# Two cross-attention layers: the negation of the maxima, the image norms, the inverse norm and the mask moved between engines

## What is computed

```python
probs_t = softmax(einsum('bhsd,bhtd->bhst', q, k_t) * attn_scale)     # 371 text rows
attn_scores = einsum('bhsd,bhnd->bhsn', q, k_ip) * attn_scale         # 4 image rows
qsem = _l2norm(einsum('bhst,bte->bhse', probs_t, text_ehs))           # x / max(|x|, 1e-12)
ip_n = _l2norm(ip_ehs)
sem = einsum('bhse,bne->bhsn', qsem, ip_n)
probs_ip = softmax(attn_scores + 0.5 * sem) * spatial_mask[None, None, :, None]
ip_out = einsum('bhsn,bhnd->bhsd', probs_ip, v_ip)
out = (text_out + ip_out) @ W_out + b_out + residual
```

## Time and profile before

| what | value |
|---|---|
| median of 3 runs | 2812.94 us (2812.1 to 2813.39) |
| the profiled execution | 2810.17 us, of which the span from the first to the last instruction is 2808.4 us |
| PE (matmul) busy | 2666.7 us, 95% |
| DVE busy | 1709.4 us, 61% |
| ACT busy | 1253.6 us, 45% |
| POOL busy | 468.7 us, 17% |
| granted TensorE clock, mean | 0.988 |

### The profile page before, as it was taken

The page is one execution under the profiler, slowest core; times in us unless marked ns, Lnnn a source line. Parts: engine busy times, 40 slices in busy tenths (PEclk is TensorE's granted clock), DMA queues, the critical chain, the costliest instruction groups (busy, mean ns, idle before and its releaser), DMA issues.

```text
span 2808.4 us, 61414 instructions
## 1 busy us (share of the span) xinstructions
PE 2666.7 (95%) x25096; PEld 2083.7 (74%) x25096; DVE 1709.4 (61%) x3464; ACT 1253.6 (45%) x2265; POOL 468.7 (17%) x681
## 2 busy tenths in 40 slices
PE   6899999999999999999999999999999999999977
PEld 5677777777777777777777777777777777777755
DVE  3465666765666755666755666655666655667654
ACT  2344444444444444444444444444444444444443
POOL 1111121111121111121111111111111111111100
PEclk8999999999999999999999999999999999999988
DMA  7576546665546765546764556674557665567630
GB/s 196 97 85 87 83 80 83 90 85 84 84 78 84 93 85 81 82 76 90 88 90 79 83 77 86 83 98 76 82 80 88 84 91 80 83 83 85 85 35 7
DMA packets 450078, 236.31 MB, mean 84 GB/s; under 512 B 220459, under 2 KB 449787, under 8 KB 449788
## 3 DMA queue, kind: packets, MB, share of 16 engines
q1 hardware_dynamic: 433958, 209.34, 55.9%
q10 hardware_dynamic: 15840, 23.04, 2.7%
HBM read 166.38 MB, written 64.59 MB: 82 GB/s over the span
## 4 chain that ended last, share of the span: by engine, by line
PE 76%; DVE 13%; SPq 3%; ACT 3%; DMA 3%; issue 2%; POOL 0%; DVEq 0%; ACTq 0%; POOLq 0%
PE R L715 7%; PE ST L672 6%; PE R L569 5%; PE PN L689 5%; PE PN L745 5%; PE R L559 4%; PE R L616 4%; PE PN L732 4%; DVE m L899 4%; PE R L565 3%; PE R L718 3%; PE R L720 3%; PE R L629 3%; PE R L630 3%; PE R L766 2%
## 5 line engine op out<-in xcount | busy, mean ns | idle before, releaser
L1133 ACT ACTIVATE p<-ST 128x1344 f32<-128x1344 f32 x320 | 413.3, 1291 | 155.3 <-PE ST L675 149.5
L715 PE MATMUL R<-pr,Gh 128*128 128x448 f32 (+1 forms) x960 | 369.9, 385 | 28.4 <-DVE acc L801 28.4
L804 DVE SCALAR_TENSOR_TENSOR w<-p,pr 128x1344 f32<-128x1344 f32 x160 | 249.3, 1558 | 227.0 <-ACT pr L1148 227.0
L801 DVE TENSOR_TENSOR rem<-R,kst 128x375 f32<-128x375 f32 (+1 forms) x160 | 87.6, 547 | 485.2 <-ACT kst L1028 485.2
L801 DVE TENSOR_TENSOR w<-R,w 128x448 f32<-128x448 f32 (+1 forms) x480 | 290.7, 622 | 104.0 <-PE R L720 95.5
L629 PE MATMUL R<-wvh,ch 128*128 128x320 f32 (+3 forms) x896 | 302.8, 338 | 11.2 <-DVE cl L801 10.9
L630 PE MATMUL R<-wvh,cl 128*128 128x320 f32 (+3 forms) x896 | 279.6, 312 | 0.0
L672 PEld LDWEIGHTS ST<-Qs,Ks 100*128 100x128 bf16 (+1 forms) x3520 | 189.1, 98 | 88.0 <-issue 32.9
L1194 POOL TENSOR_TENSOR kst<-rem,kst 128x375 bf16<-128x375 f32 (+1 forms) x160 | 146.6, 916 | 618.7 <-ACT kst L1028 319.9
L672 PE MATMUL ST<-Qs,Ks 100*128 100x112 bf16 (+1 forms) x3520 | 228.7, 214 | 15.5 <-DMA Qs<-ms 6.8
L1148 ACT ACTIVATE pr<-ST 128x1344 fp32r<-128x1344 f32 x160 | 205.3, 1283 | 82.2 <-PE R L720 82.2
(11 more groups left out here) (178 smaller groups left out, 5761.7 us busy)
## 6 DMA issues: line engine op xcount, KB each, us to landing
Ks<-k_split SPq DMA_DIRECT2D x384, 140.6 KB, 6.4
k_split<-kst SPq DMA_DIRECT2D x128, 281.2 KB, 3.1
Ks<-k_split SPq DMA_DIRECT2D x384, 93.8 KB, 9.4
Qs<-q_split SPq DMA_DIRECT2D x384, 70.0 KB, 9.2
cT<-in_ctxT ACTq DMA_DIRECT2D x30, 750.0 KB, 4.7
q_split<-qst SPq DMA_DIRECT2D x128, 84.0 KB, 2.0
k_split<-kst SPq DMA_DIRECT2D x64, 140.6 KB, 2.9
xT<-in_xT SPq DMA_DIRECT2D x32, 192.0 KB, 3.2
```

The source lines that it names most:

```text
L715: e.matmul(r[0:nj, 0:QW], Gh[0:ROWS[u], q:q + nj], pr[0:ROWS[u], QW * u:QW * u + QW], start=u == 0, stop=False)
L801: return e.tensor_tensor(to, x, y, op)
L804: return e.scalar_tensor_tensor(out=to, in0=x, scalar=s, in1=y, op0=op0, op1=op1)
L1133: e.activation(p32[i][:].rearrange("p (u q) -> p u q", u=3), st, ACT.Exp).then_inc(p_whole, 1)
```

## The change

Four edits. (1) The stage's DVE instruction `m_neg` and the tile `mn` go; PE transposes `m0` or `m1` directly once the eighth reduction is done, and ACT's two copies scale by -1. (2) The inverse image norms are multiplied into the columns `g4` by POOL in stage `w4`, before ACT spreads them; DVE's multiplication L998 goes. (3) ACT's `Sqrt` and DVE's reciprocal L994 go; POOL raises `d2` to the power -0.5 in stage `ns_T`, and a constant factor moves into `ninv`. (4) Mask and inverse sum are applied in one `scalar_tensor_tensor`, and L1014 goes.

```diff
-                    w.wait_ge(m_neg, at("m_neg", b, l))
-                    e.transpose(R[slot["R", ("m_T", b, l)]][0:n, 0:S], mn[:, 0:n], ident[0:S, 0:S]).then_inc(m_T, 1)
+                    w.wait_ge(s_max_read, 8 * at("m_T", b, l))
+                    e.transpose(R[slot["R", ("m_T", b, l)]][0:n, 0:S], (m0, m1)[l][:], ident[0:S, 0:S]).then_inc(m_T, 1)
...
-                    e.tensor_scalar(nv, nv, 0.5, None, ALU.mult).then_inc(dve_step, own.one())
+                    e.tensor_scalar(nv, nv, 0.5 / math.sqrt(2.0), None, ALU.mult).then_inc(dve_step, own.one())
...
-                    if at("s_max", *key) > 8:
-                        w.wait_ge(m_neg, (at("s_max", *key) - 1) // 8)
+                    if h0 == 0 and ("m_T", (b - 1, l)) in o.nth:
+                        w.wait_ge(m_T, at("m_T", b - 1, l))
...
-                    e.tensor_scalar(mn[:, 0:n], m_[:], -1.0, None, ALU.mult).then_inc(m_neg, 1)
...
-                    w.wait_ge(d_root, b + 1)
-                    e.reciprocal(sm[0][:], d2[:]).then_inc(dve_step, own.one())
-                    w.wait_ge(dve_step, own.n)
-                    tt(f0[:], num[:], sm[0][:].unsqueeze(2).to_broadcast([S, H, NIP]), ALU.mult).then_inc(num_read, 1)
+                    w.wait_ge(d_inverse, b + 1)
+                    tt(f1[:], num[:], d2[:].unsqueeze(2).to_broadcast([S, H, NIP]), ALU.mult).then_inc(num_read, 1)
                     w.wait_ge(num_read, b + 1)
-                    tt(f1[:], f0[:], ninv[0:S, b, :].unsqueeze(1).to_broadcast([S, H, NIP]), ALU.mult).then_inc(
-                        dve_step, own.one())
-                    w.wait_ge(dve_step, own.n)
...
-                    e.tensor_scalar(sm[0][:], sm[2][:], side[:, 0:1], None, ALU.mult).then_inc(dve_step, own.one())
-                    w.wait_ge(dve_step, own.n)
                     if b:
                         w.wait_ge(ip_T, b)
-                    tt(f1[:], f0[:], sm[0][:].unsqueeze(2).to_broadcast([S, H, NIP]), ALU.mult).then_inc(ip_weights, 1)
+                    stt(f1[:], f0[:], side[:, 0:1], sm[2][:].unsqueeze(2).to_broadcast([S, H, NIP]), ALU.mult,
+                        ALU.mult).then_inc(ip_weights, 1)
...
# ACT
-                    w.wait_ge(g_hi, at("g", b, 2))
+                    w.wait_ge(g4_scaled, b + 1)
...
-                    copy(mrem[0:n, :], r[0:n, 0:S])
-                    copy(ms[0:n, 0, :], r[0:n, 0:S]).then_inc(m_hi, 1)
+                    copy(mrem[0:n, :], r[0:n, 0:S], -1.0)
+                    copy(ms[0:n, 0, :], r[0:n, 0:S], -1.0).then_inc(m_hi, 1)
...
-                elif kind == "ns_T":
-                    b, = key
-                    w.wait_ge(d_bound, b + 1)
-                    e.activation(d2[:], d2[:], ACT.Sqrt, scale=2.0).then_inc(d_root, 1)
...
# POOL
+                if kind == "w4":
+                    b, = key
+                    w.wait_ge(g_hi, at("g", b, 2))
+                    w.wait_ge(v_mask, 1)
+                    e.tensor_tensor(g4[:], g4[:], ninv[:, b, :].unsqueeze(1).to_broadcast([128, 3, NIP]),
+                                    ALU.mult).then_inc(g4_scaled, 1)
...
+                elif kind == "ns_T":
+                    b, = key
+                    w.wait_ge(d_bound, b + 1)
+                    if b:
+                        w.wait_ge(num_read, b)
+                    e.tensor_tensor(d2[:], d2[:], minus_half[:].to_broadcast([S, H]), ALU.pow).then_inc(d_inverse, 1)
```

More of the change, by code:

```diff
@@ L1 @@
+import math
 from contextlib import ExitStack
@@ L138, in m_rows @@
     def m_rows(b, l):
-        o.add("m_neg", b, l)
         yield
@@ L425, in xattn_two_layers @@
         m1 = sb("m1", [S, H])
-        mn = sb("mn", [S, 2 * H])
         mrem = sb("mrem", [2 * H, S])
@@ L441, in xattn_two_layers @@
         side = sb("side", [S, 1])
+        minus_half = sb("minus_half", [S, 1])
         ident = sb("ident_sb", [128, 128])
@@ L464, in xattn_two_layers @@
         c_hi, parts_dve, parts_pool = (sem(n) for n in ("c_hi", "parts_dve", "parts_pool"))
-        g_mm, g_hi, g_lo, w4_copied = (sem(n) for n in ("g_mm", "g_hi", "g_lo", "w4_copied"))
-        s_max_mm, s_max_read, m_neg, m_T, m_hi, m_low = (
-            sem(n) for n in ("s_max_mm", "s_max_read", "m_neg", "m_T", "m_hi", "m_low"))
+        g_mm, g_hi, g_lo, g4_scaled, w4_copied = (sem(n) for n in ("g_mm", "g_hi", "g_lo", "g4_scaled", "w4_copied"))
+        s_max_mm, s_max_read, m_T, m_hi, m_low = (
+            sem(n) for n in ("s_max_mm", "s_max_read", "m_T", "m_hi", "m_low"))
         s_mm, p_whole, p_round, w_made = (sem(n) for n in ("s_mm", "p_whole", "p_round", "w_made"))
@@ L471, in xattn_two_layers @@
             sem(n) for n in ("y_mm", "w_times_y", "ns_mm", "ns_read", "ns_T", "ns_sum"))
-        d_bound, d_root, fused, fus_less, ip_exp, ip_weights, ip_T, ip_T_copied, ip_mm, ip_added, num_read = (
-            sem(n) for n in ("d_bound", "d_root", "fused", "fus_less", "ip_exp", "ip_weights", "ip_T", "ip_T_copied",
+        d_bound, d_inverse, fused, fus_less, ip_exp, ip_weights, ip_T, ip_T_copied, ip_mm, ip_added, num_read = (
+            sem(n) for n in ("d_bound", "d_inverse", "fused", "fus_less", "ip_exp", "ip_weights", "ip_T", "ip_T_copied",
                              "ip_mm", "ip_added", "num_read"))
@@ L1196, in gpsimd @@
             for kind, key in o.stages:
-                if kind == "start":
+                if kind == "w4":
[4 more added lines that the diff above has]
+                                    ALU.mult).then_inc(g4_scaled, 1)
+                elif kind == "start":
                     for t_ in Ks:
@@ L1204, in gpsimd @@
                     e.memset(g4[:], 0.0)
+                    e.memset(minus_half[:], -0.5)
                     e.memset(x1T[:], 0.0).then_inc(pool_set, 1)
```

## The result

| | before | after |
|---|---|---|
| median | 2813.16 us (4 runs, 2812.1 to 2814.58) | 2939.82 us (4 runs, 2930.85 to 2944.23) |
| ratio | | 1.0447, 95% interval 1.0427 to 1.0467 |
| profiled execution, its span | 2810.17, 2808.4 us | 2937.53, 2935.7 us |
| granted TensorE clock, mean | 0.988 | 0.964 |

What follows compares the result with a forecast made beforehand. PE's own work fills most of a period, DVE bounds a stretch of some 8 us. Ordinary items saved 11.5 us, late ones lost 8.5, overlap returned 1.9, negation 6.0: 10.9 us, so 2802, range 2784 to 2848.

Steps and rivals of the forecast that it cites:

- I take 1.0 us: Assumed duration of POOL's power on 20 columns, put at 19 subtractions' worth per column; no row showed a power.
- The line through the subtractions: POOL subtractions of 112 and 512 columns: 2.2 ns per column on 0.145 us, so at least 0.19 us for 20 columns.
- the dear row: POOL's 1.27 us subtraction of 512 columns, taken for a dear power and doubled to 2.5 us for the range.
- a still dearer power: Case beyond the range's upper end, a power longer than 2.5 us; chance 0.13.
- The stall model: DVE waits for POOL's power by its duration P less 0.79 us: 0.92 free, 0.13 for handovers.
- The queue: POOL must do `vbd`, which waits for a DMA, before the power; late in every item as a rival: 2826, chance 0.05.
- late items: 12 of the first 30 items, where `vbd` ends after `d2`, by 1.35 us in the mean, delaying the power.
- the prediction's own sum: Savings of 18 ordinary and 12 late items, plus returned overlap 1.9 and negation 6.0: 10.9 us at a 1.0 us power.
- The dear power as a rival: Each microsecond of the power costs 30 us: 2832 at 2.0 us, 2847 at 2.5; chance 0.32.
- The negation, 6 us,: PE's transpose of the maxima no longer waits for DVE's negation: 0.2 us per period, times 30.
- The table loads at nothing: Two ACT table loads of 1.28 us per period lie beside other work; on the path as a rival: 2731, chance 0.02.
- the fold on POOL at nothing: Image norms on POOL take 0.2 us; ACT's later spreading is hidden by 2.22 us idle, without that cover 17 us.

Runs made afterwards that it cites:

- e1: Changed kernel with ACT's square root and DVE's reciprocal back in place of POOL's power, the other three edits kept: 2796.06 us, ratio 0.9934.
- e5: Changed kernel with PE doing the first Gram product of each item twice, where it waits for DVE: 2895.2 us, ratio 1.0269.
- e3: Changed kernel with a multiplication by -0.5 in place of the power, the inverse norm left out: 2793.93 us, ratio 0.9925.
- e11: Kernel before with only the image norms folded into the four columns by POOL: 2801.78 us, ratio 0.9956.
- e8: Changed kernel with POOL's block mask behind the power instead of ahead of it: 2942.08 us, ratio 1.0436.
- e7: Changed kernel with the stages from fuse on dealt out two reductions later: 2946.02 us, ratio 1.045.

## Why the prediction was wrong, by its own steps

- **"I take 1.0 us"** is the step that failed. No row or run gives that figure; the power takes 3.54. The line through the subtractions was right for a multiplication (0.22 us), and the dear row, even doubled to 2.5, was no bound, as the prediction said itself; the range was still built on it. What two sizes of a subtraction give is the price of a subtraction's column: 2.2 ns, where a column of the power takes 157. The result lies in the branch that the prediction called a still dearer power and gave 0.13.
- **The stall model held.** P - 0.79 gives 2.75 us at the measured P; DVE's wait was 2.73 in ordinary items. The queue was as seen: 13 of 32 items had `vbd` behind `d2`, up to a wait of 4.34. For all items the model gives 2.75 x 32 = 88, and with the prediction's 12 late items at 1.35 us more 104 us; measured were 102.2.
- **The clock had no term.** With P = 3.54 the prediction's own sum is -1.90 x 18 - 3.25 x 12 + 7.9 = -65 us, so 2878. Measured was 62 more. Some 51 of that is the clock: that is the rest over e1, and in e5 the same matmuls took 45 us less (PE's busy time rose by 27 where the extra ones take 72). Some 6 of the other 11 are DVE's waits in the last two items (2.73 and 3.64 us), for which the sum had no term. The model was linear in P, and PE's idle time turned it: with 10 columns the rest is 18 us, with 20 it is 51.
- **The dear power as a rival** (0.32) had the right sign and mechanism; its price, 30 us per microsecond, is the stall alone. From 10 to 20 columns, 1.57 us, the kernel lost 84.5 us, 54 per microsecond.
- **The other terms** held together: 24 us at the measured price of a multiplication, 21 in e3. Edits 1, 2 and 4 alone were worth (0.28 + 0.27 + 0.2) x 30 = 22 us by the prediction and gave 17. The fused instruction did end with `cl`, as forecast.
- **The negation, 6 us,** was mis-sized: 3 us (1 to 6). I looked for the wait removed and not for the one behind it.
- **The table loads at nothing, the fold on POOL at nothing:** right, as far as e3 and e11 can tell.

Left open: the rest of 9 us in e5, whose mean clock is that of e1, and how the clock's share splits between items.

## What to carry to other kernels

When an operation that the trace doesn't show is put on the critical chain, measure it first on its real shape; two sizes of another operation on the same engine don't bound it. When a stall lands on a nearly always busy PE, look for two costs: the stall, and matmuls behind it at the lower clock. Here a wait that grew by 42 us brought 17 us of the second, and one that grew by 93 us brought 51. Filling the gap with extra matmuls tells the two apart and here returned a third of the loss. And a slot freed on one engine helps only if no other engine's instruction then runs beside it and is held by it, as DVE's multiplication was in e8.

## What the runs showed of the hardware

- POOL's power of fp32: 1.97 us for 112x10, 3.54 us for 112x20, the same within 0.03 us in all items; a multiplication of the same shape 0.22.
- A DVE instruction with two SBUF inputs that starts while POOL's `tensor_tensor` runs on the block mask or on `cl` ends just behind it: `fus<-num,d` took 0.81 us instead of 0.24 beside the 0.79 us block mask (e8), 1.3 beside a 1.26 us subtraction (e7), and `zq<-zs` 0.64 instead of 0.17 beside the block mask (item 15 of the changed kernel). The Trainium skill (Advanced Engine Details and Errata, GPSIMD Details) names the read and write interface that POOL shares with DVE. These rows agree. Whether the power itself holds such an instruction, no run here shows.
- PE fell to 1.2 GHz behind waits of 2.14, 0.30 and 0.56 us within one item, and was back at 2.4 GHz from about 1541.6 us on. It fell in 26 places of the changed kernel between 200 and 2740 us, against 2 of the kernel before and 3 of e5, whose longest wait for DVE there is 1.0 us.
